# FFN zero points: negated once at the start, added to the loaded weights by the transfer itself, and one more down column taken by ScalarE and added by GpSimd

## The reference, cut to what matters

```python
def dequantize(imatrix, scales, zeros, group_size, out_dtype):
    rs = jnp.repeat(scales, group_size, axis=0)
    rz = jnp.repeat(zeros, group_size, axis=0)
    return ((imatrix.astype(rs.dtype) - rz.astype(rs.dtype)) * rs).astype(out_dtype)
...
gate = jax.nn.silu(jnp.dot(x, gate_proj))
up = jnp.dot(x, up_proj)
return jnp.dot(gate * up, down_proj)
```

## Time and profile before

| | us |
|---|---|
| median of 3 runs (lowest, highest) | 834.75 (834.3, 835.59) |
| the profiled execution | 834.15 |
| its span in the profile | 832.3 |
| TensorE busy, clock granted | 818.4 (98%), 0.998 |
| VectorE, ScalarE, GpSimd busy | 562.2, 535.6, 549.8 |

### The profile page before, as it was taken

How to read it: one execution, slowest core, us unless ns; L and a number is a source line. 1 busy time by engine, 2 the same in 40 slices (tenths; PEclk the granted TensorE clock), 3 DMA queues, 4 the chain that set the end, 5 groups by cost and what they waited for, 6 DMA issues and landing times. The chain is left out here.

```text
span 832.3 us, 13342 instructions
## 1 busy us (share of the span) xinstructions
PE 818.4 (98%) x3952; PEld 674.8 (81%) x3952; DVE 562.2 (68%) x993; ACT 535.6 (64%) x1773; POOL 549.8 (66%) x555
## 2 busy tenths in 40 slices
PE   9999999999999999999999999999999999999996
PEld 7887888888778888888888888888887777777775
DVE  5516755433666666666666666666568899999997
ACT  4633652245777777777777777777677477677774
POOL 3432642322677777777777777777677268999997
PEclk9999999999999999999999999999999999999999
DMA  9412666105666666666667766666754024443312
GB/s 318 157 38 59 159 172 195 50 1 151 185 190 197 189 187 186 186 187 186 187 188 228 227 188 179 202 183 190 239 152 152 1 76 152 152 152 134 117 53 102
DMA packets 96199, 130.02 MB, mean 156 GB/s; under 512 B 25792, under 2 KB 68672, under 8 KB 96128
## 3 DMA queue, kind: packets, MB, share of 16 engines
q1 hardware_dynamic: 95696, 128.39, 51.4%
q10 hardware_dynamic: 432, 0.79, 0.3%
HBM read 90.08 MB, written 39.06 MB: 155 GB/s over the span
## 5 line engine op out<-in xcount | busy, mean ns | idle before, releaser
L1685 PE MATMUL pair<-split,xnT_hi 128*128 128x512 f32 x288 | 112.6, 391 | 0.3 <-issue 0.3
L1687 PE MATMUL pair<-split,xnT_lo 128*128 128x512 f32 x288 | 112.1, 389 | 0.0
L1686 PE MATMUL pair<-split,xnT_hi 128*128 128x512 f32 x288 | 112.1, 389 | 0.0
L1025 ACT ACTIVATE headT<-land,wqk 128x512 f32<-128x512 f32 x62 | 44.9, 724 | 92.3 <-DMA land<-block_bounce 78.4
L1685 PE MATMUL pair<-split,aoT_hi 128*128 128x512 f32 x244 | 95.9, 393 | 0.5 <-DVE resid L1485 0.5
L1687 PE MATMUL pair<-split,aoT_lo 128*128 128x512 f32 x244 | 95.3, 391 | 0.0
L1686 PE MATMUL pair<-split,aoT_hi 128*128 128x512 f32 x244 | 94.9, 389 | 0.0
L1853 PE MATMUL pair<-xnT_hi,split 128*128 128x512 f32 x224 | 90.7, 405 | 2.0 <-DVE kv L1606 1.2
L1036 ACT ACTIVATE prob<-pair,nmax 128x128 f32<-128x128 f32 x244 | 85.9, 363 | 9.5 <-DVE nmax L1461 9.2
L771 POOL TENSOR_TENSOR prob<-prob,rinv 128x512 f32<-128x512 f32 x61 | 63.6, 1043 | 38.4 <-DVE rinv L1432 38.4
L1854 PE MATMUL pair<-xnT_lo,split 128*128 128x512 f32 x224 | 87.6, 391 | 0.0
(11 more groups left out here) (202 smaller groups left out, 2161.9 us busy)
## 6 DMA issues: line engine op xcount, KB each, us to landing
block_bounce<-tb SPq DMA_DIRECT2D x244, 128.0 KB, 2.3
land<-block_bounce SPq DMA_DIRECT2D x61, 512.0 KB, 3.4
raw<-in_wqo_dram SPq DMA_DIRECT2D x62, 256.0 KB, 3.0
kv<-in_ffn_w_dram SPq DMA_DIRECT2D x14, 768.0 KB, 4.4
kv<-in_ffn_z_dram SPq DMA_DIRECT2D x14, 768.0 KB, 5.6
kv<-key_bounce SPq DMA_DIRECT2D x32, 128.0 KB, 2.8
key_bounce<-tb SPq DMA_DIRECT2D x44, 64.0 KB, 2.1
resid<-in_x_dram SPq DMA_DIRECT2D x2, 1024.0 KB, 8.6
```

The lines of the kernel that those rows point to most:

```text
L1685: pe.matmul(dst, l_hi, r_hi, start=first, stop=False)
L1686: pe.matmul(dst, l_hi, r_lo, start=False, stop=False)
L1687: return pe.matmul(dst, l_lo, r_hi, start=False, stop=last)
```

## The change

The zero points are loaded once, as 21504 whole numbers spread over 128 partitions (168 each). GpSimd negates them in two steps (zero minus zero, then minus zero), SP stores them to `negated_zeros` in device memory and only then loads the context, which uses the same place on chip. A unit is now loaded as its weights alone, in one of four slots instead of two pairs; GpSimd issues a second transfer of the same size that reads the unit's row of negated zero points 128 times and **adds** it to the weights in their slot (`accum_op=ALU.add`). The three subtractions per unit are gone, and ScalarE converts the weights where they were loaded. E2 moves from `V_POS` to `A_POS`: ScalarE takes it into `tmp_c` behind the rounding of `hidden`, and GpSimd adds it.

```diff
@@ the tables
-        FIRST_UNITS = {30: (0, 0), 33: (0, 1), 50: (1, 0), 52: (1, 1)}
+        FIRST_UNITS = {30: 0, 36: 1, 54: 2, 56: 3}
-        V_POS, A_POS = (1, 2, 4, 5, 7, 8, SIDE), (0, 3, 6, 9)
+        V_POS, A_POS = (2, 4, 5, 7, 8, SIDE), (0, 1, 3, 6, 9)
@@ SP, start
+                    sp.dma_start(zero, zeros_flat(ffn_z)).then_inc(s_zl, 16)
...
             for c in range(WQ0, WFFN):
                 weights(c, c + 1)
+                if c == WKEY - 2:
+                    sp.wait_ge(s_zn, 2)
+                    sp.dma_start(zeros_flat(zneg_scr), zneg).then_inc(s_zs, 16)
                 if c == WKEY - 1:
+                    sp.wait_ge(s_zs, 16)
                     sp.dma_start(ctxn, ctx.rearrange("b p d -> p b d")).then_inc(s_ctxn, 16)
@@ SP, units
+            def load_unit(n):
+                sp.dma_start(unit_raw(n).bitcast(I32), ffn_w[n]).then_inc(s_uw[n % SLOTS], 16)
...
+            for n in range(SLOTS, UNITS):
+                sp.wait_ge(s_uu, n - SLOTS + 1)
+                sp.wait_ge(s_ud, n - SLOTS + 1)
+                load_unit(n)
@@ GpSimd, start
             ln_rstd(0, 1)
+            pool.wait_ge(s_zl, 16)
+            pool.tensor_tensor(zneg, zero, zero, ALU.subtract).then_inc(s_zn, 1)
+            pool.wait_ge(s_zn, 1)
+            pool.tensor_tensor(zneg, zneg, zero, ALU.subtract).then_inc(s_zn, 1)
@@ GpSimd, units
+            def zeros_off(n):
+                if n == 0:
+                    pool.wait_ge(s_zs, 16)
+                pool.wait_ge(s_uw[n % SLOTS], 16 * (n // SLOTS + 1))
+                pool.dma_start(unit_raw(n).bitcast(I32), zneg_scr[n:n + 1, :].to_broadcast([P, UW]), accum_op=ALU.add)\
+                    .then_inc(s_uz[n % SLOTS], 16)
...
             def unit(i, p):
-                more = p is not None or i < LAST
-                sub_down(i, p)
                 hidden_lo(i - 1, p)
-                if more:
-                    sub_gate(i + 1, p)
-                if p is not None or i >= 3:
+                if i >= 3:
+                    add_down(i - 2, p, 2)
                     add_down(i - 2, p, 3)
-                if more:
-                    sub_up(i + 1, p)
+                if i + 2 < UNITS:
+                    zeros_off(i + 2)
                 if p is not None or i >= 2:
                     add_down(i - 1, p, 0)
...
-                if j == STEPS - 10:
-                    sub_gate(0, None)
-                if j == STEPS - 9:
-                    sub_up(0, None)
-                if j == STEPS - 8:
-                    sub_down(0, None)
+                if j in (STEPS - 16, STEPS - 13):
+                    zeros_off((j - STEPS + 16) // 3)
@@ ScalarE
             def gate_ready(i, p):
-                act.wait_ge(s_sg, unit_at(p, i) + 1)
+                act.wait_ge(s_uz[i % SLOTS], 16 * (i // SLOTS + 1))
...
                 take(i, p, 0, gated(par), gu_s[:, par, 0:1])
                 hidden_hi(i - 1, p)
+                if not skipped(i, p, 1):
+                    if i == 2:
+                        act.wait_ge(s_ds, 1)
+                    elif i >= 4:
+                        act.wait_ge(s_p2, n - 3)
+                    take(i, p, 1, accT[:, 2, :] if i == 2 else tmp_c, down_s[:, par, 2:3])
                 up_ready(i, p)
...
                 if p is not None or i >= 2:
-                    act.wait_ge(s_tv, by_vector(n, 1))
+                    act.wait_ge(s_tv, by_vector(n - 1, SIDE))
                 down_ready(i, p)
@@ VectorE
                 dve.wait_ge(s_gs, n + 1)
-                if not skipped(i, p, 1):
-                    take_down(i, p, 1, 2, p is None and i == 2)
```

67 lines of the change are left out of this document (25 added, 42 removed).

## The result

| | before | after |
|---|---|---|
| median | 835.1 us (834.3 to 835.59, 4 runs) | 857.36 us (855.63 to 858.73, 4 runs) |
| ratio to before, 95% interval | | 1.0265 [1.025, 1.0279] |
| profiled execution | 834.15 us, span 832.3 us | 855.63 us, span 853.8 us |

A forecast was written before the change was run, and what follows sets the result against it. TensorE is busy 98%; in the last stage VectorE sets the unit's 11.31 us period, ScalarE's chain having 0.49 us slack. 834.15 + 6.5 (FFN) + 4.2 (start) = 844.85 profiled, median 845.4; 8-in-10 range 840 to 853.

The forecast's parts named there:

- the term of 6.5: FFN stage: ScalarE's extra take makes U1 0.54 us late in twelve units, period 11.85 against 11.31; +6.5 us, bounds 5 to 7.2.
- No further loss, but close: FFN bank pairs: TensorE's G3 waits for ScalarE's take of E2, yet U0's product comes just before ScalarE wants it; no cost.
- the gap: Start: the fourth wq0 block waits behind the zero points' store, so TensorE starts q products at 34.5; +4.2 us, bounds 3.5 to 6.
- I count 0 and put up to 2 in the range: Start: a drop to 1.2 GHz is possible at TensorE's idle gap; counted 0, up to 2 us in the range.
- TensorE was full through the like loads and subtractions before; 0, bounds 0 and 2.: Attention: two adding transfers with their issues come, subtractions of steps 54 to 56 go; cost 0, bounds 0 to 2 us.
- 7 assumed: Adding transfer's time from issue to landing: 7 us, bounds 4.4 to 11.2, hidden with about 3 us left.
- Rival 1: Adding transfer or its issue too slow: 863 to 880 if landing takes 14, 852 if issue takes 3; 15% in all.
- 1 to 1.5 was taken: GpSimd's issue of an adding transfer: likeliest near 1 to 1.5 us, bounds 0.46 and 4.8, hidden up to 2.4.
- Rivals 2 to 4: Only ScalarE's loop costs, 841.2 (8%); only the start costs, unit faster, 834.7 (7%); both losses hide, 830.5 (4%).
- a handoff of 0.06: FFN stage: ScalarE-to-VectorE handoff of 0.06 instead of 0.03 us, giving the upper bound of 7.2 us for the unit's loss.

The follow-up runs named there:

- Run 2: Changed kernel with the take of E2 given back to VectorE and GpSimd's add of it gone, adding transfers kept: 848.78 us, ratio 1.018.
- Run 10: Changed kernel with both weight conversions moved out from between ScalarE's rounding of hidden and its take of U0: 854.15 us, ratio 1.0245.
- run 4: Changed kernel with ScalarE's take of E2 placed ahead of the rounding of hidden instead of behind it: 845.04 us, ratio 1.0133.
- run 3: Changed kernel with the adding transfers of units 0 and 1 moving only 8 of 1536 columns: 848.36 us, ratio 1.0166.
- run 8: Changed kernel with the transfers of units 0 and 1 overwriting the weights instead of adding, same size and place: 849.7 us, ratio 1.0179.
- run 1: Changed kernel with SP's wait for and store of the negated zero points issued behind the fourth wq0 block's load: 849.46 us, ratio 1.0192.
- run 9: Kernel of run 5 with units 0 and 1 by subtractions, no adding transfer among the bounces, plain loads of units 2 and 3 later: 831.76 us, ratio 0.9962.
- run 5: Changed kernel with the edits of run 1 and run 4 together: 839.87 us, ratio 1.0056.
- run 7: Kernel of run 5 with the whole adding transfers of units 0 and 1 ten and seven steps earlier: 840.79 us, ratio 1.0083.
- run 6: Kernel of run 5 with the attention stage's 768 KB transfers cut in three pieces, one a step, and moved: 836.0 us, ratio 1.0021.

## Why the prediction was right and wrong

**The FFN stage: right in size, half right in cause.** 11.85 was predicted and 11.83 measured; the term of 6.5 is 6.5 in the ledger, of which 12 x 0.52 is 6.2 and the one longer period most of the rest. Run 2 shows that the take of E2 makes all of it. The prediction followed ScalarE's queue, and named the other chain only as "No further loss, but close": G3 waiting for the take of E2. Run 10 takes the queue away as a cause and the period stays, so that chain alone would have given the same: G3 starts 747.29 - 743.91 = 3.38 us after the product (3.33 was its release by the prediction), and U0's take at 5.52 instead of the 5.4 at which its product was expected. What both share, the take of E2 behind the rounding, was the thing to see; run 4 moves it and the unit runs at TensorE's pace.

**The start: the gap right, the clock counted as nothing.** 4.2 us were forecast for the gap, 4.4 came, with the steps at their places (block issued at 27.42 against 27.9, landed by 30.44 against 30.5, TensorE at 34.75 against 34.5). The lower clock, "I count 0 and put up to 2 in the range", is 2.05 in after. It was the wrong end: none of the six kernels with the gap was spared. The ledger's 6.4 to 8.1 at the first transposition are the gap and this; less the later start of the q products, the clock's part is 1.6 to 2.9 us, in four of the six above the bound of 2.

**The attention stage: the step that failed.** "TensorE was full through the like loads and subtractions before; 0, bounds 0 and 2." It lost 8.6 us: 1.2 ahead of the first adding transfer, 6.6 from there to the last transposition, 0.8 behind it. The 6.6 are three waits of TensorE for `aoT_lo` (5.1) and the lower clock behind the last of them (1.7), within 0.2. The prediction weighed the adding transfer by one question, whether it lands before its own reader; it did (7.7 us here against 7 assumed, 6.6 as the median in the FFN stage). The other question was not asked: who else has transfers under way meanwhile, and what is their reserve. The trace of before had an answer to the second. Beside the plain load at 579.35 the read of the bounce took 5.7 us instead of 3.4 without a wait of TensorE; anything above that was unknown ground, and an adding transfer gave 7.0. "The like loads" were not like. Runs 3 and 8 show it: without the adding (run 8) or with eight columns of it (run 3), and with all else in place, 7.7 to 9.0 us come back. How the second of the two losses arises stays open, as said at run 3.

A smaller part of the 8.6 lies behind the last attention step. A third adding transfer, which the prediction did not count, stands among the last reads of the bounce; from the last transposition to unit 0 run 1 loses 3.5 us and run 9, where it comes after them, 0.7. After itself lost 0.8 there, so this part is a matter of how they meet.

**The rivals.** Rival 1 (transfer or issue too slow for its reader) did not come: GpSimd's issue takes 0.86 us in the FFN stage (1 to 1.5 was taken), and the remainder of hidden still finds GpSimd idle for 1.45 us before it. Rivals 2 to 4 are excluded by the start's and the unit's measured losses. Two small slips in the working changed nothing: 4 x 2.36 is 9.44, not 9.46, and a handoff of 0.06 gives 12 x 0.57 = 6.8, not 7.2.

**The sum.** 834.15 + 6.5 + 4.2 = 844.85 was forecast for the profiled execution. With 6.4 for the start (gap 4.4, clock 2.0) and 8.6 for the attention stage it is 855.65, against 855.63. That is no proof, since 6.4, 8.6 and 6.5 are cut out of the measured difference; it shows where the missing 11 us are: 2.2 at the start and 8.6 in the attention stage. The median of after, 857.36, is another 1.7 us up, which no trace here explains.

On the page that the prediction weighed: run 8 against after is the comparison it needed. With the adding transfer the stretch moves 198 GB/s where it moves 324 with the plain one, 0.61 of it (0.71 from issue to landing, 220 against 310), and the transfer lands in 7.7 us against 5.3. The Trainium skill ("Collectives: The Full Stack", part on why ReduceScatter is half of AllGather) says half the rate for a reduce-scatter, since two sources are read. The trace agrees in kind, and the measured figure is milder; the two reads themselves no run here shows. What that rule would have warned of is not the transfer's own lateness but the engines it fills.

## What to carry to other kernels

A transfer has two prices: when it lands, and what it does to the transfers beside it. Before moving work from a compute engine into a transfer, list who else is transferring in that stretch, and read from the trace the longest time that one of those has taken without making the busiest engine wait; a stage whose matmuls wait on a round trip through memory has no other reserve.

Work given to an idle engine goes to a place in its queue, not to its idle time: ask which waiting gap that place is in front of. Here one place earlier made the difference between 11.83 and 10.88 us a unit. And a store whose data comes late does not belong in a queue ahead of a load that is needed early.

## What the runs showed of the chip that I had not expected

- An adding transfer keeps the transfer engines as busy as a plain one (0.95) at 198 instead of 324 GB/s, and the reads of the bounce beside a whole one land in 6.7 to 9.2 us instead of about 3.4 (after and runs 1, 5, 7 and 10). It depends on how they meet: in after the read issued 1 us ahead of the second one landed in 4.5.
- Its time has a large part that doesn't depend on its size: 4 KB landed in 4.3 and 5.4 us (run 3), 256 KB in 5.5 (run 6, median of 8), 768 KB in 7.1 to 9.6 among bounces.
- GpSimd's own operations are slower while it has just issued one: the product that takes 1.03 us took 1.35, a 128x4 add 0.49 instead of 0.20 (after, at 574.9 and 575.9; run 8, without adding, shows 1.03 and 0.20).
- A gap of 4.7 to 5 us in TensorE's work at 30 us was followed by the lower clock in all six kernels that have it. Shorter waits go either way. That of 2.43 us at 587 in after was not followed by it (clock 1.00 in 585 to 590). Those of 2.15 us at 632 in after, of 2.04 and 2.42 us in run 5 and of 2.43 us in run 7 were, and each fall takes 1.7 to 3.4 us of full speed, about as much as the wait itself. In run 1 waits of 0.85 and 0.90 us, close together, were followed by it as well (0.74 in 635 to 640). So a late transfer can cost twice: once as the wait and once as the clock.
